# Layer two of an attention kernel: the weighted values of two units as one block, the second maximum tile in front of its job

## The reference, cut to what matters

```python
x = x + _L1_xattn_ref(_layernorm(x, axis=-1), ctx_1024, ctx_1024, ...)

# inside: 16 heads of width 8
Q = _split_heads(queries @ W_q.T + b_q, H)
K = _split_heads(keys @ W_k.T + b_k, H)
V = _split_heads(values @ W_v.T + b_v, H)
scores = jnp.einsum('bhqd,bhkd->bhqk', Q, K) / jnp.sqrt(jnp.asarray(d, Q.dtype))
attn = jax.nn.softmax(scores, axis=-1)
out = jnp.einsum('bhqk,bhkd->bhqd', attn, V)
return out @ W_o.T + b_o
```

## Time and profile before

| | before |
|---|---|
| median of 3 runs | 1431.8 us (1426.97 to 1435.11) |
| the profiled execution | 1426.79 us |
| its span in the profile | 1424.7 us |
| PE, PEld, DVE busy | 89%, 74%, 75% of the span |
| ACT, POOL busy | 59%, 62% |
| layer two, steps 1 to 12 (first QP to last) | 982.00 to 1203.65 us |

### The profile page before, as it was taken

How to read it: one execution, slowest core, us unless ns; L and a number is a source line. 1 busy time by engine, 2 the same in 40 slices (tenths; PEclk the granted TensorE clock), 3 DMA queues, 4 the chain that set the end, 5 groups by cost and what they waited for, 6 DMA issues and landing times. The chain is left out here.

```text
span 1424.7 us, 44434 instructions
## 1 busy us (share of the span) xinstructions
PE 1271.9 (89%) x16309; PEld 1054.9 (74%) x16309; DVE 1072.4 (75%) x3393; ACT 838.4 (59%) x1590; POOL 882.7 (62%) x949
## 2 busy tenths in 40 slices
PE   2689999999999999379999999668999999968998
PEld 0377787787777787279999999536777788746776
DVE  4678999989989996547766666457888888835774
ACT  3167777777777767156666666235666666634552
POOL 6346888888878856547777777534554444125660
PEclk9799999999999999689999999779999999968999
DMA  6776677777777760535555555487888888534784
GB/s 185 218 218 205 220 248 245 238 242 241 239 230 233 223 189 31 192 56 64 66 65 66 64 65 64 95 235 222 259 266 268 259 263 243 158 80 115 185 186 139
DMA packets 212638, 252.15 MB, mean 177 GB/s; under 512 B 38328, under 2 KB 173752, under 8 KB 205400
## 3 DMA queue, kind: packets, MB, share of 16 engines
q1 hardware_dynamic: 179768, 226.33, 52.7%
q0 software_dynamic: 25840, 21.71, 10.9%
q10 hardware_dynamic: 6816, 1.29, 0.5%
HBM read 156.73 MB, written 91.46 MB: 174 GB/s over the span
## 5 line engine op out<-in xcount | busy, mean ns | idle before, releaser
L876 DVE TENSOR_REDUCE L_neg_max<-L_ps_mx 128x2 f32<-128x496 f32 (+1 forms) x768 | 489.4, 661 | 100.9 <-PE L_ps_mx L1062 98.5
L725 ACT ACTIVATE L_p<-L_ps_sc 120x512 f32<-120x512 f32 (+1 forms) x768 | 417.5, 598 | 207.3 <-PE L_ps_sc L1044 203.7
L1062 PE MATMUL L_ps_mx<-stack_k,stack_q 118*128 118x248 bf16 (+1 forms) x2048 | 299.1, 250 | 42.7 <-DMA stack_q<-L_q_rows 26.1
L1044 PE MATMUL L_ps_sc<-stack_q,stack_k 122*120 122x128 bf16 (+1 forms) x3072 | 300.2, 221 | 3.7 <-ACT L_p L725 2.5
L1044 PEld LDWEIGHTS L_ps_sc<-stack_q,stack_k 122*120 122x120 bf16 (+1 forms) x3072 | 239.5, 123 | 56.8 <-issue 35.4
L1563 POOL DMA_INDIRECT routed_out<-M_y,M_x x135 | 212.0, 1570 | 87.8 <-DVE M_y L1654 86.8
L1086 PE MATMUL L_ps_o<-L_p,L_v 120*18 120x128 f32 (+1 forms) x6144 | 220.8, 276 | 2.5 <-ACT L_o_sb L754 2.1
L1062 PEld LDWEIGHTS L_ps_mx<-stack_k,stack_q 118*128 118x128 bf16 x2048 | 141.7, 100 | 103.4 <-issue 35.1
L1086 PEld LDWEIGHTS L_ps_o<-L_p,L_v 120*18 120x18 f32 (+1 forms) x6144 | 147.7, 98 | 37.7 <-issue 24.7
L1433 POOL DMA_INDIRECT routed_in<-R_xn,R_slot x128 | 127.0, 993 | 42.2 <-issue 36.2
L1609 ACT COPY M_w<-stack_k 128x768 f32 x135 | 112.1, 832 | 53.6 <-PE M_ps_g L1586 36.3
(11 more groups left out here) (211 smaller groups left out, 2150.3 us busy)
## 6 DMA issues: line engine op xcount, KB each, us to landing
L_q_rows<-L_q_parts_sb SPq DMA_DIRECT2D x192, 192.0 KB, 4.1
stack_q<-L_q_rows SPq DMA_DIRECT2D x189, 192.0 KB
stack_k<-L_k_rows SPq DMA_DIRECT2D x93, 372.0 KB
stack_k<-L_k_rows SPq DMA_DIRECT2D x96, 180.0 KB
F_spread<-F_gate_rows SPq DMA_DIRECT2D x32, 512.0 KB, 7.1
L_k_rows<-L_k_parts_sb SPq DMA_DIRECT2D x32, 372.0 KB, 4.3
M_x<-routed_in SPq DMA_DIRECT2D x135, 66.0 KB, 2.0
L_k_rows<-L_k_parts_sb SPq DMA_DIRECT2D x32, 180.0 KB, 4.3
```

Source lines behind the costliest of these rows:

```text
L725: nc.scalar.activation(p_t[t][u % 2][:, quarter * 4 * S:(quarter + 1) * 4 * S], ps_sc[n % NSC][0:KEYS[t], :], ACT.Exp).then_inc(sc_read, 1)
L876: nc.vector.tensor_reduce(neg_max[:, b, kk * HPB:(kk + 1) * HPB], v, AX.X, ALU.max, negate=True).then_inc(max_read, 1)
L1044: last = mm(ps_sc[n % NSC][0:KEYS[t], j * S:(j + 1) * S], k_st[p][:, b // 2, h, b % 2, k0:k0 + KEYS[t]], q_st[p][:, b // 2, h, b % 2], sta ...
L1062: last = mm(ps_mx[i % NMX][:, j * NK:(j + 1) * NK], q_st[p][0:TERM_TOP, b // 2, h, b % 2], k_st[p][0:TERM_TOP, b // 2, h, b % 2], start=Tr ...
```

## The change

In layer two the weighted values no longer follow the second scores of each unit. They are formed in even units alone, between the first maximum tile and the second scores, and there for the two units before at once. The second maximum tile stands in front of the second job. Nothing is added or removed; the second edit moves something only where a second job exists.

```diff
     else:
         UNIT = [
-            ("job", 0), ("scores", 0), ("max", 0), ("scores", 1), ("values", 0), ("values", 1), ("job", 1),
-            ("max", 1),]
+            ("job", 0), ("scores", 0), ("max", 0), ("values", 0), ("scores", 1), ("max", 1), ("job", 1),]
...
+    PAIRED_VALUES = not first
...
+                        elif what == "values" and PAIRED_VALUES:
+                            if u % 2 == 0 and i == 0 and gp.exists:
+                                for quarter in range(2):
+                                    weighted_values(gp, up - 1, quarter)
+                                for quarter in range(2):
+                                    weighted_values(gp, up, quarter)
                         elif what == "values" and gp.exists:
                             weighted_values(gp, up, i)
```

## The result

The changed kernel has a median of 1438.3 us (1432.61 to 1445.52, 20 runs) against 1432.6 us (1426.97 to 1441.31, 20 runs): a ratio of 1.0042, interval 1.0023 to 1.0060, or 6 us slower. I had forecast 1428, 4 us faster. The profiled execution took 1434.56 us.

A forecast was written before the change was run, and what follows sets the result against it. PE was read as the bound, DVE 13% behind and transfers as much. Steps 8 to 12 -0.4, 13 and 14 -2.3, 1 to 7 -1: -3.7, 1426.79 to 1423.1 profiled; 1428 against the median, range 1418 to 1440.

The forecast's parts named there:

- Theory A: Experiments' reading of the prediction's walk: two chains of DVE, each a little longer than before, swallow what PE saves.
- OB to OP: Steps 8 to 12, emptying of OB to output projection: 4.30 us becomes 4.44, a loss of 0.14 waiting for AT.
- OP to QP: Steps 8 to 12, output projection to next query projection: 8.51 us becomes 8.61, a loss of 0.10 from gapless DVE.
- 0.91 (two blocks of 0.35, and 0.21 once): Time of the paired values block on PE in an even unit, within a pair going from 3.06 to 2.75 us.
- QP to OB: Steps 8 to 12, query projection to OB: 5.91 us becomes 5.59, a gain of 0.32, with DVE having little there.
- the 1.24 should come out nearly whole: Steps 13 and 14, where DVE's chains lose links: PE's 1.24 us saving per step nearly all kept, -2.3 for both.
- Theory B: Experiments' rival reading: the rows of maxima that ACT sends into the stack of queries come too late.
- MT later by one tile costs nothing in the same way: ACT's part: the MT job standing one maximum tile later adds no time, put at nothing.
- The one on the slower side: DVE falls behind in odd units, so XT copy and QP come late: 0.6 per step, +9, 1441 us; chance 0.17.
- Rival 1: DVE holds up better, only the chain of transfers holds: -8.3, 1423.5 us; chance 0.17.
- Rival 2: Nothing holds, the transfer chain shrinks along with PE, 15 steps give 1.24 each: -18.6, 1413 us; chance 0.08.
- Rival 4: The change does nothing, as the idle 0.21 stands before any following load: 1432 us; 0.58 together with the forecast.

The follow-up runs named there:

- the second alone: The kernel before with only the second maximum tile moved ahead of the second job, values unpaired: ratio 1.0013 (0.9993 to 1.0032).
- the first alone: The kernel before with only the values paired, the MT job staying ahead of the second maximum tile: ratio 1.0024 (1.0005 to 1.0044).

## Why the prediction was wrong

**Theory A's part, 2.1 us.** The steps "OB to OP" and "OP to QP" were right in mechanism and in size. The step that failed is the sum that gives the even unit 1.88, by its term "0.91 (two blocks of 0.35, and 0.21 once)". A unit of values within a block costs 0.44 us, not 0.35: four groups of four matmuls, each 0.11 after the last. In 0.35 the 16 loads of a single block are done, since two of their four groups start at once, and I took it for their pace. Taken from the single block of 0.56, that leaves 0.12 to save where I had 0.21; behind the block the maximum tile follows after 0.27 instead of 0.22; the way in was right (0.31). An even unit is 2.01 us and an odd one 0.88 (1159.62 to 1160.50), a pair 2.89 for 3.06: 0.17 saved, not 0.31. In unit 0 the MT job takes back half of that: it stands 0.30 behind a maximum tile now, where other pieces stand 0.22, and before it lay behind the block. The scores behind QP and the KP job took 0.02 and 0.04 more than before. So QP to OB gave 0.04 and not 0.32, which does little against the 0.14 and 0.16 that DVE's chains lose: 0.26 more than this step's 18.72, and 0.42 more than its neighbours' 18.56.

**Steps 13 and 14** were forecast 2.3 us shorter and are 0.39 longer. It is the sentence "the 1.24 should come out nearly whole" that failed, in its size by the above, and in that DVE, without statistics or normalisation, still gets the tiles of an odd unit in a burst, three reductions in a row (2.0 us at 1217.42): OB to OP is 4.08 and 4.07 us there where it was 3.98 and 3.97, and OP starts 0.15 after the end of DVE's copy of AT. Only the stretch behind OP in step 13 got shorter, by 0.16; in step 14 the same stretch got longer by 0.16, and why isn't shown.

**Theory B's part, between 1.5 and 4 us, not settled.** The step that failed is a term put at nothing. The prediction says "MT later by one tile costs nothing in the same way"; it had asked who empties MT, and not what its transfer feeds. From MT to the scores of unit 4 it was 8.20 us in step 10 (1150.92 to 1159.12; 8.07 in its four neighbours) and is 7.37 (1158.54 to 1165.91). The single edits divide this: 7.89 with the second alone, 7.55 with the first alone, in steps without a wait for a transfer. So 0.52 of the 0.70 are the pairing, since of the three values blocks that lay between them one block of two units is left, and the longer wait for AT doesn't make it up; 0.18 are MT's place. What has to happen in between, copy, place in ACT's queue, two issues and a landing of 3.8 us (median, up to 5.8), did not get shorter.

That the rows are waited for more is shown: in steps 1 to 12 the waits grow from 0.9 to 2.5 us on PE and from 4.6 to 7.3 on its weight loads, and one transfer for two brings them to 0.3 and 1.1. What it costs is known only roughly. By the ratios, the change from 1.0042 to 1.0003 is 0.0039, 5.6 us, and the kernel before gets 0.0013 of such a gain itself, which leaves 0.0026 or 3.7 us to the pairing; but each of these three ratios is known to 0.002, the difference of the differences to some 0.0036, and so the 3.7 could be nothing or 9. By the profiled executions, one each, steps 0 to 12 take 250.6 us for 246.0 with two transfers and 249.4 for 246.3 with one: 4.7 less 3.1, or 1.5 us. Whether other executions of the changed kernel had waits long enough to lose clock as well, which would lie between the two numbers, isn't recorded. The 6 us measured (3.3 to 8.6 by the interval) are thus 2.1 of theory A, 0.4 of steps 13 and 14, the rows' share, and a rest in which the wait for the source tile may have a part; that rest stays open.

**The early steps** kept their 128.7 us, where I had forecast 1 us less, within the bounds that I gave. But the chain of query transfers isn't a floor at this height, as the prediction had it: with XT and AT on ACT the unpaired kernel did the same seven steps in 125.9 and 125.2 us (two transfers and one). Step 0 stayed as it was but for 0.26 us.

**The rivals.** The one on the slower side named the late XT copy. It came, by 0.30 a step; its price was put at 0.6 and more by a feedback through the transfers of queries, which did not come. Rival 1 had DVE hold up better; DVE idled more behind the blocks, as it says (12.6 us for 7.4), and its chains still ended later. Rival 2, the whole gain by the rule of the Trainium skill ("TensorEngine Tiling (Array Packing)", "Key Properties"), could not come. The trace agrees with the rule, in that the idle 0.21 stands once per pair now and not twice, but a block of twice the length gives back only 0.12 of it. Rival 4 is out by the halved idle loads.

**Two readings of less weight.** Of the 40 idle loads behind values blocks in steps 8 to 12, five stand before a maximum tile too, with DVE named as releaser (1.1 us in all), and only five before a job. And the lead of an odd unit's scores over the end of the block adds up to 1.50 by the terms given, not 1.54. Nothing in the forecast hangs on either.

**What stays open.** With XT and AT on ACT and one transfer for the rows, pairing still isn't faster: 0.9995 for 0.9976, a difference within the noise; with the rows on SP it was faster, 1.0020 for 1.0038, a difference just clear of it. So the sign of what pairing is worth without its costs isn't known. The shortest step is 17.88 us for 18.21, but steps 8 to 12 take 92.21 for 91.87, with waits in steps 1 to 12 of 7.3 us for queries (3.3 unpaired) and 3.6 for rows (0.5). That reads as if the transfers, at 0.88 of their engines in both, bound them; no run took the query chain away to show it.

## What to carry to other kernels

When work is regrouped on an engine that looks like the bound, cost the block at its pace inside, start to start in a long run, and not by the length of a short burst: here 16 loads were done in 0.35 us and 16 more took 0.44. Then ask of each small transfer whose source and reader both sit on that engine how far apart they stand, before and after: a time saved between them is taken out of the slack of the transfer. And where two engines are as close as here (92.15 and 81.19 us busy of 92.96), look at the second before saving on the first: a list of two names, XT and AT, moved a paired step by 1 us and an unpaired one by 0.35. The time of the kernel did not follow, since waits for transfers took the place of those for DVE.

## What the runs showed that I had not expected

- Value matmuls of 18 columns in four strips, at a granted clock of 1.00: the first eight weight loads of a block start at once, then four every 0.11 us; 16 are done in 0.35 us and 32 in 0.79.
- Two transfer issues in ACT's queue directly behind the copy that writes their source held it for 1.17 us, and what followed came 1.30 later; two issues beside exponentials that were already running cost nothing that was seen. Both rows in one transfer took 0.53 us of issue for 1.1 to 1.2 us.
- Behind all five waits of PE of 3.1 to 4.1 us in steps 1 to 14 of these profiles the granted clock was 0.50 for some microseconds, and behind 11 of the 14 waits of 1.9 to 2.4 us. In the profiles of the changed kernel and the kernel before no wait was longer than 1.3 us there, and the clock stayed at 1.00.
- Where a transfer of two rows stood in SP's queue behind 4.94 us of other issues, PE waited 3.3 and 3.7 us for rows at one place of step 14 (unpaired and paired, copies by DVE), and steps 13 and 14 took 4.7 to 6.4 us more than the 33.35 before.
